# First graph layer: one product sum of 16 tiles a round, its turning and adding put into the next round

## The chip, the cores and the metric

One core of one Trainium2 chip runs the whole kernel. The metric is the device time of one execution in microseconds (us); lower is better. The engines are TensorE (PE, with its weight loads PEld), VectorE (DVE), ScalarE (ACT), GpSimd (POOL) and SyncE (SP), each with its own instruction stream; they meet at semaphores.

## The reference

Four graph layers run one after the other on 6250 nodes of 128 features and 206250 edges, sorted by destination node, and each ends in a residual add and a layer norm. Only the first layer (a graph attention layer with 4 heads of 32 channels) is touched:

```
h = (x @ W).reshape(n, 4, 32)
a_s = einsum('nhc,hc->nh', h, att_src);  a_d = einsum('nhc,hc->nh', h, att_dst)
e = leaky_relu(a_s[src] + a_d[dst], 0.2)
m = segment_max(e, dst);  p = exp(e - m[dst]);  z = segment_sum(p, dst)
out = segment_sum(h[src] * (p / z[dst])[:, :, None], dst)
```

## The kernel before

Edges are cut into tiles of 128 and rounds of 16 tiles; a round is 4 slots (b = 0 to 3) of 4 tiles. There are 101 rounds. All edges of a round fall on fewer than 128 neighbouring nodes, so the `narrow` branches run, and the rounds are written out one after another (`straight`). `par` is the round's number modulo 2.

- GpSimd (L621) fetches 16 tiles of source rows from the table in HBM by indirect DMA, into `g[par]`. The 16 DMAs of slot b = 0 to 3 wait for the product sum `agg` of the same slot of the round now finished: round i's sums free the buffer for the rows of round i + 2.
- ScalarE copies the 16 x 4 source scores of a round out of `g` into `alpha` (L727, after `g_ready`), and TensorE transposes them into `raw` (L671, semaphore `raw_t`).
- VectorE then makes the running maximum over each node's edges with scans, in steps that go back and forth between it and TensorE: scans L789 and L790, ends of tiles L792 and L793; TensorE L675; carries between tiles L799 to L804; TensorE L681; copy L809, scans L810 and L811, maximum L813; TensorE transposes it back (L689, L690); scores and weights L818 to L829. `seg` counts VectorE's steps, `carry_mm` counts TensorE's four answers of a round (L675, L681, L690, L697).
- In the gaps between these steps VectorE makes one-hot matrices (L749 for the next round's destination scores, L756 for the sums), and TensorE the next round's destination scores, `dst_scores(i + 1, b)`, L639: 4 matmuls a slot, one slot behind each of the four steps. A float32 matmul shows as two rows in the trace, so a slot is "x8".
- ScalarE exponentiates the weights (L729, L731, L732) and copies the destination scores (L720). VectorE multiplies the rows by the weights (L761, `messages`), and takes the rescale factors of the old sums from TensorE's L697 (L835).
- TensorE sums the round with one-hot matrices (L660, 4 matmuls a slot, `agg` after each). Slots 0 and 1 go into one half of a PSUM bank, 2 and 3 into the other. ScalarE copies each half to `by_node` (L738), TensorE turns it (`turn(i, h)`, L646 and L647), and VectorE adds it to the accumulator (`add_half`: L771 twice, with the rescaling, for h = 0; L768 for h = 1). All of this is done before the next round's L671 on TensorE and L789 on VectorE: turn(i, 0) stands between the sums of slots 2 and 3, turn(i, 1) behind them.
- SyncE loads the next rounds' destination rows (L572, 1 MB), windows (L538) and break marks (L578, L580).

Of the kernel before, what the change touches and what calls it, by code (L numbers as in the profile page):

```python
# [19 lines left out]
ALU = mybir.AluOpType  # L20
# [3 lines left out]
P = 128  # L24
N = 6250
E = 206250
KT = 4
SLOTS = 4
ROUND = KT * SLOTS
# [21 lines left out]
Z0 = 2 * H0 + 1  # L51
# [57 lines left out]
def build(nc, a, out):  # L109
    ctx = ExitStack()  # L110
    with ctx:
# [452 lines left out]
        def seg_base(i):  # L564
            return (i + 1) * STEPS

        with nc.Block() as block:
# [58 lines left out]
            def _(pe):  # L626
# [3 lines left out]
                def program(narrow):  # L630
# [12 lines left out]
                    def turn(i, h):  # L643
                        pe.wait_ge(node_copied, 2 * i + h + 1)
                        pe.wait_ge(acc_step, 3 * i + 7 + h)
                        nc.tensor.transpose(PS[0][:, h, 0:P], by_node[:, h, 0:P], ident[:, :])  # L646
                        nc.tensor.transpose(PS[0][0:Z0, h, P:2 * P], by_node[:, h, P:GW], ident[:, :]).then_inc(turned, 1)  # L647

                    def sums(i, b, par):
                        n = i * SLOTS + b  # L650
                        pe.wait_ge(oh_done, n + 1)
                        pe.wait_ge(msg_done, n + 1)
                        pe.wait_ge(weighed, 2 * i + 2)
                        if not narrow:
                            sum_bank_free(pe, acc_step, i, b, narrow)
                        for k in range(KT):
                            o, row_ = oh[:, b, k, :], g[:, par, b * KT + k, :]
                            bank, c, start, stop = sum_place(narrow, b, k)
                            if narrow:
                                m = nc.tensor.matmul(PS[1][:, bank, 0:GW], o, row_, start=start, stop=stop)  # L660
                            else:
                                nc.tensor.matmul(PS[bank][:, 0, c:c + P], row_[:, 0:P], o, start=start, stop=stop)
                                m = nc.tensor.matmul(PS[bank][0:Z0, 1, c:c + P], row_[:, P:GW], o, start=start, stop=stop)
                        m.then_inc(agg, 1)

                    def round_(j, i, par, last):
                        base = seg_base(i)
                        pe.wait_ge(alpha_kept, i + 1)
                        pe.wait_ge(seg, base)
                        met(pe, i)  # L670
                        nc.tensor.transpose(raw, alpha[:, :, :].rearrange(flat_q), ident[:, :]).then_inc(raw_t, 1)  # L671

# [3 lines left out]
                        if not last:  # L676
                            dst_scores(i + 1, 0)

# [22 lines left out]
                        for b in range(SLOTS):  # L701
                            sums(i, b, par)
                            if narrow and b == 2:
                                turn(i, 0)
                        if narrow:
                            turn(i, 1)

                    for b in range(SLOTS):
                        dst_scores(0, b)
                    rounds(pe, round_, narrow)  # L710
# [3 lines left out]
            def _(act):  # L714
# [7 lines left out]
                def program(narrow):  # L722
                    def round_(j, i, par, last):
                        for b in range(SLOTS):
                            act.wait_ge(g_ready[par][b], 16 * KT * (j + 1))
                        act.wait_ge(seg, seg_base(i))
                        nc.scalar.copy(alpha, g[:, par, :, P:P + H0]).then_inc(alpha_kept, 1)  # L727
                        act.wait_ge(seg, seg_base(i) + 20)
# [4 lines left out]
                        if not last:  # L733
                            keep_dst_scores(i + 1)
                        if narrow:
                            for h in range(2):
                                act.wait_ge(agg, i * SLOTS + 2 * h + 2 + AHEAD)
                                nc.scalar.copy(by_node[:, h, :], PS[1][:, h, 0:GW]).then_inc(node_copied, 1)  # L738

                    keep_dst_scores(0)  # L740
                    rounds(act, round_, narrow)
# [3 lines left out]
            def _(dve):  # L745
# [17 lines left out]
                def program(narrow):  # L763
                    def add_half(at, i, h):
                        dve.wait_ge(turned, 2 * i + h + 1)
                        dve.wait_ge(acc_step, 3 * i + 8 + 2 * h)
                        if h:
                            dve.tensor_tensor(at, at, PS[0][:, 1, 0:2 * P].rearrange("p (a n) -> p a n", a=2), ALU.add).then_inc(acc_step, 1)  # L768
                            return
                        for d in range(2):  # L770
                            dve.scalar_tensor_tensor(at[:, d, :], at[:, d, :], scale2[:, d:d + 1], PS[0][:, 0, d * P:(d + 1) * P], ALU.mult, ALU.add).then_inc(acc_step, 1)  # L771
# [8 lines left out]
                    def round_(j, i, par, last):  # L780
# [25 lines left out]
                        between(i, 1, last)  # L806

# [26 lines left out]
                        dve.wait_ge(carry_mm, 4 * i + 4)  # L834
                        s.link(dve.tensor_tensor(scale2, down_p, unit2[:, :], ALU.add))  # L835
# [3 lines left out]
                        if narrow:  # L839
                            at = acc2[:, :, bass.ds(first_node(dve, i * ROUND), P)]  # L840
                            for h in range(2):
                                add_half(at, i, h)
                            return
# [1468 lines left out]
```

## Time and profile before

| | |
|---|---|
| median of 3 runs | 11816.71 us (11815.05 to 11828.76) |
| profiled execution | 11788.6 us, span 11786.7 us |
| busy: PE, PEld, DVE, ACT, POOL | 55%, 47%, 41%, 15%, 52% |
| mean granted TensorE clock | 0.639 of full speed |

The profile is of one execution. Its page divides the span into 40 slices of about 295 us; the rounds of the first layer lie in the first eleven. PE records are starts of matmuls and modelled ends. "Idle" in a row is the time its engine did nothing before it, with what ended it; "remote" means a semaphore whose sender the profile doesn't name there, "issue" nothing that it shows.

### The profile page before, as it was taken

The page shows a single profiled execution, that of the slowest core. Times are in us where ns is not written, and L with a number is a line of the kernel's source. Part 1 is how long each engine was busy: PE and PEld are TensorE (multiplying, and loading weights), DVE is VectorE, ACT ScalarE, POOL GpSimd, SP SyncE. Part 2 cuts the span into 40 slices and gives each one's busy share as a digit, 9 for nine tenths or more (in the row PEclk, how much of TensorE's full clock was granted, in tenths as well). Part 3 has the DMA queues.
Part 4 walks back from the last instruction along what each step waited for, and adds up shares of the span by engine and source line. Part 5 has one row for each costly group of instructions (what it writes and reads, how often), then busy time and mean ns, then how long its engine had stood idle before and what let it go on. Part 6 is the DMA issues. An engine that isn't in the chain of part 4 may idle for free. (4 is left out here: it accounts for less than half of the span.)

```text
span 11786.7 us, 95611 instructions
## 1 busy us (share of the span) xinstructions
PE 6487.3 (55%) x31067; PEld 5541.6 (47%) x31067; DVE 4881.6 (41%) x10538; ACT 1784.6 (15%) x2785; POOL 6158.0 (52%) x6479
## 2 busy tenths in 40 slices
PE   4555555555435555555544445444443677777775
PEld 4444444444425555555434444444432455555553
DVE  4444444444552222222345555555555344444444
ACT  0000000000110000000110000000011444444443
POOL 4544544554216666666445555555530566666663
PEclk6666666666555555555566666666655677777776
DMA  4222222222111111111133433333320222222221
GB/s 132 72 75 74 73 75 75 72 75 75 42 26 55 54 55 55 54 55 54 44 123 121 124 121 119 121 120 122 120 69 1 65 62 61 61 60 61 62 61 38
DMA packets 388329, 878.63 MB, mean 75 GB/s; under 512 B 134341, under 2 KB 202872, under 8 KB 368224
## 3 DMA queue, kind: packets, MB, share of 16 engines
q0 software_dynamic: 232704, 536.56, 16.5%
q1 hardware_dynamic: 150242, 324.95, 8.3%
q10 hardware_dynamic: 4896, 11.01, 0.2%
q8 instruction: 258, 4.23, 0.1%
q14 instruction: 229, 1.88, 0.1%
HBM read 839.65 MB, written 32.40 MB: 74 GB/s over the span
## 5 line engine op out<-in xcount | busy, mean ns | idle before, releaser
L621 POOL DMA_INDIRECT PM<-gat_table,src_idx x1616 | 1529.1, 946 | 1579.9 <-PE ps L660 1070.4
L2081 POOL DMA_INDIRECT TMP<-schnet_table,src_idx x1616 | 1563.3, 967 | 1355.5 <-DVEq L2183 481.8
L1595 POOL DMA_INDIRECT PM<-hgt_kv_table,src_idx x1616 | 1531.4, 948 | 1371.3 <-PE ps L1627 752.0
L1153 POOL DMA_INDIRECT PM<-gcn_table,src_idx x1004 | 953.0, 949 | 463.8 <-issue 288.6
L1169 PE MATMUL ps<-rows,xT 16*128 16x8 f32 x3232 | 625.6, 301 | 716.3 <-issue 696.0
L1169 PEld LDWEIGHTS ps<-rows,xT 16*128 16x128 f32 x3232 | 646.2, 277 | 702.8 <-issue 671.7
L1153 POOL DMA_INDIRECT TMP<-gcn_table,src_idx x612 | 578.6, 945 | 702.4 <-POOLq L1016 373.9
L2108 PE MATMUL ps<-PM 128*128 128x128 f32 x3232 | 627.8, 357 | 539.6 <-issue 402.7
L2108 PEld LDWEIGHTS ps<-PM 128*128 128x128 f32 x3232 | 571.7, 266 | 582.3 <-issue 581.9
L1627 PE MATMUL ps<-PM 128*128 128x136 f32 x3232 | 608.8, 353 | 337.5 <-DVE PM L1716 322.1
L1228 DVE TENSOR_TENSOR AC<-AC,ps 128x128 f32 x101 | 29.2, 289 | 1829.8 <-remote 1437.0
L639 PE MATMUL ps<-PM 128*128 128x4 f32 x3232 | 697.6, 339 | 101.9 <-issue 71.9
L1627 PEld LDWEIGHTS ps<-PM 128*128 128x128 f32 x3232 | 557.8, 253 | 374.6 <-DVE PM L1702 345.1
L639 PEld LDWEIGHTS ps<-PM 128*128 128x128 f32 x3232 | 662.3, 304 | 134.1 <-issue 90.1
L1610 PE MATMUL ps<-TMP 128*128 128x128 f32 x3232 | 654.2, 367 | 59.0 <-issue 24.4
L660 PE MATMUL ps<-PM 128*128 128x137 f32 x3232 | 644.2, 377 | 0.3 <-issue 0.3
L1610 PEld LDWEIGHTS ps<-TMP 128*128 128x128 f32 x3232 | 585.5, 271 | 91.0 <-issue 37.8
L2153 DVE TENSOR_TENSOR PM<-ps,TMP 128x512 f32<-128x512 f32 x404 | 277.2, 686 | 830.9 <-remote 609.4
L660 PEld LDWEIGHTS ps<-PM 128*128 128x128 f32 x3232 | 618.7, 281 | 3.0 <-issue 0.3
L2091 PE MATMUL ps<-PM,WA 50*128 50x512 f32 x808 | 595.3, 825 | 11.1 <-DMA PM<-in_attrT 11.1
L689 PE MATMUL ps<-ident,TMP 64*128 64x64 f32 x101 | 36.8, 365 | 1011.3 <-DVE TMP L813 844.4
L2098 PEld LDWEIGHTS ps<-WA,PM 128*128 128x128 f32 x3232 | 566.2, 246 | 35.8 <-issue 14.8
(374 smaller groups left out, 10772.4 us busy)
## 6 DMA issues: line engine op xcount, KB each, us to landing
PM<-local_dst_row SPq DMA_DIRECT2D x101, 1024.0 KB
PM<-local_dst_row SPq DMA_DIRECT2D x202, 512.0 KB
PM<-in_attrT SPq DMA_DIRECT2D x101, 400.0 KB
PM<-gat_table,src_idx POOLq DMA_INDIRECT x1616
PM<-hgt_kv_table,src_idx POOLq DMA_INDIRECT x1616
TMP<-schnet_table,src_idx POOLq DMA_INDIRECT x1616
PM<-gcn_table,src_idx POOLq DMA_INDIRECT x1004
xT<-in_rel_row SPq DMA_DIRECT2D x101, 128.0 KB
```

The costliest lines, as they stand in the source:

```text
L621: pool.indirect_dma_start(out=g[:, par, t, 0:ROW0], out_offset=None, in_=tab0_d, in_offset=bass.IndirectOffsetOnAxis(ap=src_idx[:, i * ROU ...
L639: m = nc.tensor.matmul(adp[:, t * H0:(t + 1) * H0], ohT[:, b % 2, k * P:(k + 1) * P], window_of(narrow, adw, i, b, k), start=True, stop=True)
L660: m = nc.tensor.matmul(PS[1][:, bank, 0:GW], o, row_, start=start, stop=stop)
L1153: pool.indirect_dma_start(out=g[n % DEEP][:, k, :], out_offset=None, in_=tab1_d, in_offset=bass.IndirectOffsetOnAxis(ap=src_idx[:, n * KT ...
L1169: m = nc.tensor.matmul(rel_ps[par][:, t, :], oh16[kind_rows(par), t * P:(t + 1) * P], rel_rows[kind_rows(par), :], start=True, stop=True)
L1595: pool.indirect_dma_start(out=g[:, par, t, 0:2 * P], out_offset=None, in_=kv_d, in_offset=bass.IndirectOffsetOnAxis(ap=src_idx[:, i * ROUN ...
L1610: m = nc.tensor.matmul(q_ps[b % 2][:, k, :], ohT[:, b % 2, k * P:(k + 1) * P], window_of(narrow, qw, i, b, k), start=True, stop=True)
L1627: m = nc.tensor.matmul(sums_ps, o, row_, start=b % 2 == 0 and k == 0, stop=b % 2 == 1 and k == KT - 1)
L2081: pool.indirect_dma_start(out=g[:, b, k, :], out_offset=None, in_=tab3_d, in_offset=bass.IndirectOffsetOnAxis(ap=src_idx[:, (i * SLOTS + b ...
L2091: nc.tensor.matmul(zb[b], w1, attr[:, par, b * KT * P:(b + 1) * KT * P], start=True, stop=True).then_inc(z_mm, 1)
L2098: m = nc.tensor.matmul(wb[b % 2][:, k, :], soft[:, b % 2, k * P:(k + 1) * P], w2, start=False, stop=(k == KT - 1), skip_group_check=True)
L2108: m = nc.tensor.matmul(sb_[bank][:, c:c + P], msg[:, b % 2, k, :], oh[:, b % 2, k, :], start=start, stop=stop)
```

## The change

The four slots of a round are summed into one PSUM region (`PS[1][:, par]`) as one sum of 16 tiles; ScalarE copies it once, `turn` and the add are done once a round. They move into the next round: TensorE's `turn(i - 1)` stands behind L675 and `dst_scores(i + 1, 0)`, VectorE's `add_round(i - 1)` behind its second `between` and ahead of the wait of L809. The transposition of the next round's scores (`scores_t(i + 1)`, with its wait for `alpha`) stands between the sums of slots 1 and 2, and ScalarE copies the next round's `alpha` (`keep_alpha`) before it waits for the sums. VectorE waits for the previous round's add before it writes the new rescale factors (L835). The last round turns and adds at its own end.

```diff
-                    def turn(i, h):
-                        pe.wait_ge(node_copied, 2 * i + h + 1)
-                        pe.wait_ge(acc_step, 3 * i + 7 + h)
-                        nc.tensor.transpose(PS[0][:, h, 0:P], by_node[:, h, 0:P], ident[:, :])
-                        nc.tensor.transpose(PS[0][0:Z0, h, P:2 * P], by_node[:, h, P:GW], ident[:, :]).then_inc(turned, 1)
+                    def turn(i, par):
+                        pe.wait_ge(node_copied, i + 1)
+                        pe.wait_ge(acc_step, 2 * i + 6)
+                        nc.tensor.transpose(PS[0][:, par, 0:P], by_node[:, par, 0:P], ident[:, :])
+                        nc.tensor.transpose(PS[0][0:Z0, par, P:2 * P], by_node[:, par, P:GW], ident[:, :]).then_inc(turned, 1)
+
+                    def scores_t(i):
+                        pe.wait_ge(alpha_kept, i + 1)
+                        pe.wait_ge(seg, seg_base(i))
+                        met(pe, i)
+                        nc.tensor.transpose(raw, alpha[:, :, :].rearrange(flat_q), ident[:, :]).then_inc(raw_t, 1)
...
-                                m = nc.tensor.matmul(PS[1][:, bank, 0:GW], o, row_, start=start, stop=stop)
+                                m = nc.tensor.matmul(PS[1][:, par, 0:GW], o, row_, start=b + k == 0, stop=b + k == SLOTS + KT - 2)
...
-                        pe.wait_ge(alpha_kept, i + 1)
-                        pe.wait_ge(seg, base)
-                        met(pe, i)
-                        nc.tensor.transpose(raw, alpha[:, :, :].rearrange(flat_q), ident[:, :]).then_inc(raw_t, 1)
-
...
                         if not last:
                             dst_scores(i + 1, 0)
+                        if narrow and i > 0:
+                            turn(i - 1, 1 - par)
...
                             sums(i, b, par)
-                            if narrow and b == 2:
-                                turn(i, 0)
-                        if narrow:
-                            turn(i, 1)
+                            if b == 1 and not last:
+                                scores_t(i + 1)
+                        if narrow and last:
+                            turn(i, par)
...
-                    def round_(j, i, par, last):
+                    def keep_alpha(j, i, par):
                         for b in range(SLOTS):
                             act.wait_ge(g_ready[par][b], 16 * KT * (j + 1))
-                        act.wait_ge(seg, seg_base(i))
                         nc.scalar.copy(alpha, g[:, par, :, P:P + H0]).then_inc(alpha_kept, 1)
...
                             keep_dst_scores(i + 1)
+                            keep_alpha(j + par, i + 1, 1 - par)
                         if narrow:
-                            for h in range(2):
-                                act.wait_ge(agg, i * SLOTS + 2 * h + 2 + AHEAD)
-                                nc.scalar.copy(by_node[:, h, :], PS[1][:, h, 0:GW]).then_inc(node_copied, 1)
+                            if i >= 2:
+                                act.wait_ge(turned, i - 1)
+                            act.wait_ge(agg, i * SLOTS + SLOTS + AHEAD)
+                            nc.scalar.copy(by_node[:, par, :], PS[1][:, par, 0:GW]).then_inc(node_copied, 1)
...
-                    def add_half(at, i, h):
-                        dve.wait_ge(turned, 2 * i + h + 1)
-                        dve.wait_ge(acc_step, 3 * i + 8 + 2 * h)
-                        if h:
-                            dve.tensor_tensor(at, at, PS[0][:, 1, 0:2 * P].rearrange("p (a n) -> p a n", a=2), ALU.add).then_inc(acc_step, 1)
-                            return
+                    def add_round(i, par):
+                        at = acc2[:, :, bass.ds(first_node(dve, i * ROUND), P)]
+                        dve.wait_ge(turned, i + 1)
+                        dve.wait_ge(acc_step, 2 * i + 8)
                         for d in range(2):
-                            dve.scalar_tensor_tensor(at[:, d, :], at[:, d, :], scale2[:, d:d + 1], PS[0][:, 0, d * P:(d + 1) * P], ALU.mult, ALU.add).then_inc(acc_step, 1)
+                            dve.scalar_tensor_tensor(at[:, d, :], at[:, d, :], scale2[:, d:d + 1], PS[0][:, par, d * P:(d + 1) * P], ALU.mult, ALU.add).then_inc(acc_step, 1)
...
                         between(i, 1, last)
+                        if narrow and i > 0:
+                            add_round(i - 1, 1 - par)
...
                         dve.wait_ge(carry_mm, 4 * i + 4)
+                        if narrow:
+                            dve.wait_ge(acc_step, 2 * i + 8)
                         s.link(dve.tensor_tensor(scale2, down_p, unit2[:, :], ALU.add))
...
                         if narrow:
-                            at = acc2[:, :, bass.ds(first_node(dve, i * ROUND), P)]
-                            for h in range(2):
-                                add_half(at, i, h)
+                            if last:
+                                add_round(i, par)
                             return
```

## Rows read from the trace of the kernel before

**Rows 1.** The page, part 2: busy tenths in 40 slices of the span.
```profile
PE   4555555555435555555544445444443677777775
DVE  4444444444552222222345555555555344444444
POOL 4544544554216666666445555555530566666663
PEclk6666666666555555555566666666655677777776
```

**Rows 2.** Waits, 200 to 2900 us: waiting engine and line, releaser, total us, times, longest.
```profile
DVE TMP L809 <- remote: 862.8, 85, 12.4
POOL PM L621 <- PE ps L660: 954.8, 93, 12.3
DVE AC L771 <- PE ps L647: 212.6, 48, 4.9
DVE AC L771 <- issue: 183.2, 41, 5.2
DVE AC L768 <- PE ps L647: 108.3, 54, 3.6
DVE AC L768 <- issue: 62.2, 34, 3.5
```

**Rows 3.** Timeline, GpSimd's first fetch of the 5th and of the 99th round.
```profile
203.57 0.94 POOL L621 DMA_INDIRECT PM<-gat_table,src_idx  x1 [12.20 <-PE ps L660]
...
3061.33 0.95 POOL L621 DMA_INDIRECT PM<-gat_table,src_idx  x1 [9.81 <-PE ps L660]
```

**Rows 4.** Timeline of one round, 625 to 657 us: start, us, instruction, count, idle before.
```profile
626.29 0.95 POOL L621 DMA_INDIRECT PM<-gat_table,src_idx  x1 [9.59 <-PE ps L660]
...
629.16 1.10 PE L660 MATMUL ps<-PM 128*128 128x137 f32 x8
629.46 0.61 DVE L771 SCALAR_TENSOR_TENSOR AC<-AC,TMP,ps 128x128 f32 x2 [4.42 <-PE ps L647]
630.56 0.28 ACT L738 COPY TMP<-ps 128x137 f32<-128x137 f32 x1 [2.40 <-PE ps L660]
...
631.36 0.42 DVE L768 TENSOR_TENSOR AC<-AC,ps 128x256 f32 x1 [1.29 <-PE ps L647]
632.02 0.41 DVE L789 TENSOR_TENSOR_SCAN TMP<-PM,ps 64x128 f32<-64x128 f32 x1 [0.23 <-PE ps L671]
...
633.19 0.22 PE L675 MATMUL ps<-TMP,head_of 64*4 64x32 f32 x2 [1.76 <-DVE TMP L792]
...
633.78 1.05 PE L639 MATMUL ps<-PM 128*128 128x4 f32 x8 [0.37 <-issue]
...
634.26 0.13 DVE L799 COPY TMP<-TMP 4x1 f32<-4x1 f32 x1
...
634.78 0.28 DVE L804 TENSOR_TENSOR TMP<-TMP,ident 4x128 f32<-4x128 f32 x1
...
635.12 0.54 PE L681 MATMUL ps<-ones,TMP 4*64 4x1 f32 x4 [0.28 <-issue]
...
645.04 0.94 POOL L621 DMA_INDIRECT PM<-gat_table,src_idx  x1 [0.30 <-issue]
647.61 0.15 DVE L809 COPY TMP<-ps 64x2 f32<-64x2 f32 x1 [11.34 <-remote]
...
650.08 0.13 DVE L818 TENSOR_TENSOR TMP<-TMP,ps 4x1 f32<-4x1 f32 x1
...
653.17 0.14 DVE L835 TENSOR_TENSOR TMP<-ps,unit 128x2 f32<-128x2 f32 x1
...
656.58 0.95 POOL L621 DMA_INDIRECT PM<-gat_table,src_idx  x1 [10.60 <-PE ps L660]
```

**Rows 5.** Timeline of a round whose L675 came early, 2515 to 2546 us.
```profile
2515.55 0.95 POOL L621 DMA_INDIRECT PM<-gat_table,src_idx  x1 [12.10 <-PE ps L660]
...
2523.28 0.58 PE L681 MATMUL ps<-ones,TMP 4*64 4x1 f32 x4 [0.18 <-issue]
...
2529.82 0.15 DVE L809 COPY TMP<-ps 64x2 f32<-64x2 f32 x1 [5.40 <-remote]
...
2538.32 0.14 DVE L818 TENSOR_TENSOR TMP<-TMP,ps 4x1 f32<-4x1 f32 x1 [5.95 <-remote]
...
2544.83 0.95 POOL L621 DMA_INDIRECT PM<-gat_table,src_idx  x1 [9.53 <-PE ps L660]
```

**Rows 6.** Timeline of a round whose L681 came late, 2361 to 2396 us.
```profile
2361.05 0.95 POOL L621 DMA_INDIRECT PM<-gat_table,src_idx  x1 [9.64 <-PE ps L660]
...
2375.04 0.58 PE L681 MATMUL ps<-ones,TMP 4*64 4x1 f32 x4
...
2384.10 0.15 DVE L809 COPY TMP<-ps 64x2 f32<-64x2 f32 x1 [7.92 <-remote]
...
2393.08 0.94 POOL L621 DMA_INDIRECT PM<-gat_table,src_idx  x1 [12.27 <-PE ps L660]
```

More of the change, by code:

```diff
@@ L702, in round_ @@
                             sums(i, b, par)
-                            if narrow and b == 2:
-                                turn(i, 0)
-                        if narrow:
-                            turn(i, 1)
+                            if b == 1 and not last:
+                                scores_t(i + 1)
+                        if narrow and last:
+                            turn(i, par)
                     for b in range(SLOTS):
                         dst_scores(0, b)
+                    scores_t(0)
                     rounds(pe, round_, narrow)
@@ L722, in program, with round_ @@
                 def program(narrow):
-                    def round_(j, i, par, last):
+                    def keep_alpha(j, i, par):
                         for b in range(SLOTS):
                             act.wait_ge(g_ready[par][b], 16 * KT * (j + 1))
-                        act.wait_ge(seg, seg_base(i))
                         nc.scalar.copy(alpha, g[:, par, :, P:P + H0]).then_inc(alpha_kept, 1)
+                    def round_(j, i, par, last):
                         act.wait_ge(seg, seg_base(i) + 20)
@@ L734, in round_ @@
                             keep_dst_scores(i + 1)
+                            keep_alpha(j + par, i + 1, 1 - par)
                         if narrow:
-                            for h in range(2):
-                                act.wait_ge(agg, i * SLOTS + 2 * h + 2 + AHEAD)
-                                nc.scalar.copy(by_node[:, h, :], PS[1][:, h, 0:GW]).then_inc(node_copied, 1)
+                            if i >= 2:
+                                act.wait_ge(turned, i - 1)
+                            act.wait_ge(agg, i * SLOTS + SLOTS + AHEAD)
+                            nc.scalar.copy(by_node[:, par, :], PS[1][:, par, 0:GW]).then_inc(node_copied, 1)
                     keep_dst_scores(0)
+                    act.wait_ge(seg, seg_base(0))
+                    keep_alpha(0, 0, 0)
                     rounds(act, round_, narrow)
```

## Prediction, written before the changed kernel was built or run

> **What bounds the kernel now.** I read the page's slices first, then the waits of the first layer, then its timeline round by round. The chain that ended last is of no use here: it ends in the fourth layer. In the slices no engine of the first eleven is full: PE and GpSimd stand at 4 to 5 tenths and TensorE is granted 0.6 of its speed [rows 1]. So the layer is bound by a chain that goes from engine to engine, and its length per round is what counts. The first fetch of the 5th and of the 99th round are 3061.33 - 203.57 = 2857.76 us apart: 94 rounds of 30.40 us [rows 3].
>
> The waits say where those go. Per round VectorE waits some 10 us at the copy L809 (862.8 us, 85 times), and 6 us for the turned sums: 212.6 + 183.2 + 108.3 + 62.2 = 566 us at L771 and L768 over 89 rounds. GpSimd waits 10 us for the sums, 954.8 us in 93 waits [rows 2]. A reader who takes these at face value sees 6 us a round to win by moving the turn away. The timeline says that it is less simple.
>
> I count from the first fetch of a round (F). In the ordinary round [rows 4] F is 626.29. The turned sums hold VectorE until 631.78; the scans start at F + 5.7, L675 at F + 6.9, L681 at F + 8.8. L681's record ends at F + 9.4 and nothing else stands before the copy L809, yet this starts at F + 21.3. The fetches run from F to F + 19.7 (last at 645.04, 0.94 us). From L809 to the next F the chain takes 8.97 us, from L818 6.50 us, from L835 3.41 us.
>
> The wait at L809 is the strange part. Twelve PE rows (8 of L639's slot 0, 4 of L681) are recorded between F + 7.5 and F + 9.4, but their answer is there only at F + 21.3: from L681's start 12.5 us, or 1.04 us a row, while the fetches run. Earlier in the same fetches answers come at once: L675 at 633.19 lets L799 start at 634.26. The Trainium skill ("Perfetto Trace Analysis", Summary: the profiler window per engine type) says that a TensorE record's end is an estimate and that semaphore propagation is hidden from it; the trace agrees, since L809 comes 11.9 us after L681's recorded end.
>
> How does the wait depend on when L681 comes? In an early round [rows 5] L681 is at F + 7.7, L809 at F + 14.3: 1.1 us earlier in, 7.0 us earlier out. But then L818 waits 5.95 us, until F + 22.8, and the next F is at F + 29.3. In a late round [rows 6] L681 is at F + 14.0, L809 at F + 23.05, the next F at + 32.0. So there is a shadow over TensorE's answers from about F + 7.5 to about F + 22.8: what enters before it is prompt, what enters it crawls, and all is out soon after the fetches end. The period is the time at which the shadow lets go plus the chain that is still undone then: 21.3 + 9.0 = 30.3, 22.8 + 6.5 = 29.3, 23.05 + 9.0 = 32.0.
>
> **The change part by part.**
> Moved off the head of the round: both turns, their adds and the copies. VectorE is free for the scans as soon as the transposed scores are there. These come behind the sums of slot 1; the three slots behind the first end at 629.16 + 1.10 = F + 4.0, so slot 1 ends near F + 2 and the scans can start near F + 2.3 instead of F + 5.7. `alpha` doesn't hold it: its copy stands behind ScalarE's L720 and needs rows that were fetched a round earlier.
> But L675 stands in TensorE's queue behind the sums of slot 3, so it comes at F + 4.1, or some tenths later with the extra transposition in between, against F + 6.9. L804 comes 1.59 us behind L675 (633.19 to 634.78), lasts 0.28, and lets L681 start: F + 6.1 against F + 8.8. That is 2.7 us earlier, and out of the 6 us that the waits seemed to offer.
>
> Added before L681 on TensorE: `turn`, behind slot 0 of L639. It waits for the copy of `by_node`, which started 0.3 us behind the sums (630.56), so it is there at F + 4.6; L639's slot 0 takes 1.05 us from F + 4.5. The turn costs two transpositions, about 0.3 us by the nearest rows. If it falls in the shadow it costs its 2 to 4 rows at 1.04 us, so 2 to 4 us. I take 0.3, since it is issued near F + 5.6.
> Added before L809 on VectorE: two rows of 0.61 us together, as L771. VectorE is idle there now. If that cover goes they cost 0.61 us; queued behind are L809 to L813, and TensorE's L689 waits for those. One add of 0.42 us (L768), one copy of 0.28 us on ScalarE and two transpositions go away for good. All lie beside the wait: 0.
> The wait before L835 is for adds made some 15 us earlier: 0; were it real, the messages of slots 1 to 3 and the sums would queue behind it. DMAs: none is added or moved; SyncE's and GpSimd's lists are as before. The sums keep their 16 matmuls and an `agg` a slot, so the fetches start by the same rule.
>
> Where does the new round meet the shadow? By F + 7.5 slot 0 of L639, the turn and L681 (F + 6.1 to 6.7) are in. L809 then lies between 6.8 (prompt) and 14.3 (the early round); I take F + 8.5, nearer the prompt end since L681 is 1.6 us ahead of the early round's. What is next late is L818: it needs slot 1 of L639 (8 rows), L689 (1) and L690 (2). Eleven rows at 1.04 are 11.4 us: F + 20. The shadow's end, F + 22.8, is the upper bound. I take the middle, F + 21.4, and 6.5 us behind it: period 27.9 us.
> The sum: (27.9 - 30.4) x 100 rounds = -250 us. The bounds: L818 at F + 22.8 gives 29.3 (-110 us). If L690 too got out early, the shadow would hold slot 2 of L639 and L697, and let go at 22.8 with L835's 3.4 us to do: 26.2 (-420 us).
> The span 11786.7 becomes 11537; the profiled execution took 11788.6, 28 us less than the median of the runs, 11816.7, which becomes 11567.
>
> **The rivals.**
> *A, the full shadow (29.3 us a round, -110 us, 11707).* L818's answer is held to F + 22.8 as in the early round [rows 5]. For it: that round had L809 at 14.3 and still paid. Against: there L690 was entered about F + 16, in the new order near F + 10.
> *B, more gets through (26.2, -420 us, 11397).* Against: 11 rows would have to pass in far less than 1.04 us each.
> *C, the wait isn't tied to the fetches but to the products, and keeps its 12.5 us.* Then L809 moves with L681 by 2.7 us: 27.7, -270 us, 11547. The late round speaks against it, with 9.1 us. The Trainium skill ("SBUF — State Buffer", Who interferes with whom) says that only the port pair of VectorE and GpSimd contends and that DMA never contends with a compute engine; by that rule this rival would be the right one. No row names what holds TensorE's answers.
> *D, swallowed.* The shadow depends on how much TensorE has done since F, not on when. The new order has the same 24 rows of sums and 8 of slot 0 ahead of L681, so L809 stays at F + 21.3: 30.4, 0 us, 11817. The early round speaks against it: same work, 7 us sooner.
> *E, slower.* The turn waits in the shadow: if slot 0 of L639 is held, the turn behind it adds its 2 to 4 us ahead of L681, and VectorE's add stands ahead of L809. It decides if L681's answer comes later than F + 21.3; then L809 goes to the late round's 23.05 and the period to 32.0: +160 us, 11977. For it: the turn was prompt between the sums, and its new place is 3 us nearer to the shadow.
> The change does do what it says: the narrow branch runs, since `turn` has records.
>
> **How the numbers follow.** Forecast 0.40, A 0.15, B 0.12, C 0.11, D 0.10, E 0.12. 0.2% is 24 us, about what a measurement can tell from no change. Faster: 0.40 + 0.15 + 0.12 + 0.11 = 0.78; same 0.10; slower 0.12. The range leaves out E and a tail beyond B: 11380 to 11830; B and D lie inside. The forecast's own range is 11420 to 11680 (26.5 to 29.1 us).
>
> **What would show it.** The scans L789 should start near F + 2.3, L675 near F + 4.3, L681 near F + 6.3. The idle time before L809 should shrink from 10 us a round to 2 or 3, and that before L818 rise to 8 or more; L768 is gone; the first fetches should stand 27.9 us apart. GpSimd's wait for L660 should fall from 10 to 8 us. The other layers should be the same. I am wrong if L809 still comes at F + 21 (D, E), or if L818 does not wait and the wait has gone to L835 or the sums (B).

## The result and the profile after

The changed kernel takes 11733.34 us (median of 4, 11731.05 to 11745.68), the kernel before on the same chip 11820.16 us: ratio 0.9926, interval 0.9914 to 0.9938, 87 us less. Forecast were 250 us less (11567). The sign was right, the size was not; 87 us lies nearest to rival A (110).

The profiled execution took 11745.68 us, its span 11743.3. GpSimd's first fetches of two rounds, 92 rounds apart (for the kernel before: [rows 3]):

```profile
201.04 0.94 POOL L621 DMA_INDIRECT PM<-gat_table,src_idx  x1 [12.17 <-PE ps L666]
...
2941.93 0.94 POOL L621 DMA_INDIRECT PM<-gat_table,src_idx  x1 [12.20 <-PE ps L666]
```

2740.89 / 92 = 29.79 us a round against 30.40: 0.61 x 100 = 61 us of the 87. In these two profiled executions the second layer's first fetch comes at 3419.8 us instead of 3486.3, so 66 us earlier, but the spans differ by 43 us only: the third layer, which the change doesn't touch, took 17 us longer. About 20 us either way lies in the other layers from one execution to the next.

Lines have moved (before -> now): L671 -> L653, L789 -> L796, L675 -> L676, L799 -> L806, L681 -> L684, L809 -> L818 (the copy of the carries), L818 -> L827 (the scores), L835 -> L846. The sums are now L666, the add L778. Note that L818 names the scores in the old kernel and the copy of the carries in the new one. Below, "the carries" and "the scores" mean the moment at which VectorE goes on with TensorE's answer. One ordinary round of the changed kernel, timeline, against [rows 4]:

```profile
1512.61 0.94 POOL L621 DMA_INDIRECT PM<-gat_table,src_idx  x1 [12.18 <-PE ps L666]
...
1514.25 0.41 DVE L796 TENSOR_TENSOR_SCAN TMP<-PM,ps 64x128 f32<-64x128 f32 x1 [2.88 <-issue]
...
1516.03 0.22 PE L676 MATMUL ps<-TMP,head_of 64*4 64x32 f32 x2
1516.17 1.05 PE L639 MATMUL ps<-PM 128*128 128x4 f32 x8
...
1518.31 0.14 DVE L806 COPY TMP<-TMP 4x1 f32<-4x1 f32 x1 [1.75 <-remote]
...
1519.24 0.39 PE L684 MATMUL ps<-ones,TMP 4*64 4x1 f32 x4 [1.53 <-DVE TMP L811]
...
1524.86 0.61 DVE L778 SCALAR_TENSOR_TENSOR AC<-AC,TMP,ps 128x128 f32 x2 [4.48 <-remote]
...
1528.31 0.15 DVE L818 COPY TMP<-ps 64x2 f32<-64x2 f32 x1 [2.85 <-remote]
...
1535.38 0.14 DVE L827 TENSOR_TENSOR TMP<-TMP,ps 4x1 f32<-4x1 f32 x1 [4.52 <-remote]
...
1541.90 0.94 POOL L621 DMA_INDIRECT PM<-gat_table,src_idx  x1 [9.57 <-PE ps L666]
```

Read from the first fetch F = 1512.61: the scans start at F + 1.6, L676 at F + 3.4, L684 at F + 6.6, close to the forecast (2.3, 4.3, 6.3). But VectorE already waits 1.75 us for L676's answer, the turned sums come at F + 12.3, the carries (L818) at F + 15.7, and the scores (L827) at F + 22.8. The chain behind L827 is 6.5 us as before, and the next F is at 29.3. One long wait was cut into four. Over the 92 rounds the medians are F + 5.7 for L806, 17.2 for the carries and 22.9 for the scores; the carries range from 10.8 to 23.0, but the scores never come before F + 22.7.

The trace also keeps the time at which each semaphore was raised, which no view above prints. In this round TensorE's answers arrive in the order of its instructions: L676's at F + 5.7, the turn's at 12.1, L684's at 15.7, that of L639's slot 1 at 22.70, the scores' at 22.75 and that of slot 2 at 22.84. From L676 to L684 stand 14 matmul rows (8 of slot 0, 2 of the turn, 4 of L684): 10.0 us, so 0.7 us a row; the 8 rows of slot 1 take another 7.0 us, 0.9 us a row. Then the 8 rows of slot 2, of which each has its own record at F + 17.7 to 19.6, are answered 0.1 us behind slot 1's and the scores'. Eight such rows took 1.05 us at best here (L639 at 1516.17), so these had been computed before and only their answer was held, behind the answers ahead of it.

Some rounds take 31 to 32 us. This is the round just before the one above:

```profile
1480.73 0.95 POOL L621 DMA_INDIRECT PM<-gat_table,src_idx  x1 [9.56 <-PE ps L666]
...
1488.94 0.39 PE L684 MATMUL ps<-ones,TMP 4*64 4x1 f32 x4 [1.47 <-DVE TMP L811]
...
1503.63 0.15 DVE L818 COPY TMP<-ps 64x2 f32<-64x2 f32 x1 [2.81 <-remote]
...
1506.11 0.13 DVE L827 TENSOR_TENSOR TMP<-TMP,ps 4x1 f32<-4x1 f32 x1
```

L684 comes at F + 8.2 and the carries at F + 22.9, so the scores at 25.4: 31.9 us. Of 92 rounds 72 took 29.3 to 29.6 us, and 15 took 31.1 to 31.9. All 15 are among the 23 rounds, every fourth, at whose start SyncE also loads L578. The waits from 200 to 2900 us, against [rows 2]:

```profile
POOL PM L621 <- PE ps L666: 918.9, 93, 12.2
DVE AC L778 <- remote: 486.7, 84, 11.6
...
DVE TMP L818 <- remote: 334.9, 84, 5.7
DVE TMP L827 <- remote: 215.5, 60, 9.4
```

### The profile page after: what moved, and what is told of

It reads as the page before. It is cut to its first block and busy times, and to the rows that moved or that the text cites. A ratio compares the mean times of both kernels' runs of the same rounds, so it can differ in the third digit from the quotient of the medians.

```text
span 11743.3 us, 95003 instructions
## 1 busy us (share of the span) xinstructions
PE 6312.4 (54%) x30865; PEld 5385.9 (46%) x30865; DVE 4855.6 (41%) x10437; ACT 1759.6 (15%) x2684; POOL 6154.7 (52%) x6479
## 3 DMA queue, kind: packets, MB, share of 16 engines
q0 software_dynamic: 232704, 536.56, 17.7%
## 5 line engine op out<-in xcount | busy, mean ns | idle before, releaser
L2118 PEld LDWEIGHTS ps<-PM 128*128 128x128 f32 x3232 | 567.1, 264 | 586.1 <-issue 585.8
L1637 PEld LDWEIGHTS ps<-PM 128*128 128x128 f32 x3232 | 560.6, 254 | 342.0 <-DVE PM L1712 317.6
L639 PE MATMUL ps<-PM 128*128 128x4 f32 x3232 | 614.7, 313 | 81.4 <-DVE PM L758 59.7
L666 PE MATMUL ps<-PM 128*128 128x137 f32 x3232 | 633.8, 372 | 0.3 <-issue 0.3
L639 PEld LDWEIGHTS ps<-PM 128*128 128x128 f32 x3232 | 579.5, 269 | 107.8 <-DVE PM L758 72.4
L666 PEld LDWEIGHTS ps<-PM 128*128 128x128 f32 x3232 | 610.5, 277 | 4.1 <-issue 0.3
L2101 PE MATMUL ps<-PM,WA 50*128 50x512 f32 x808 | 587.3, 815 | 12.3 <-DMA PM<-in_attrT 12.3
```

Source lines behind the costliest of these rows:

```text
L639: m = nc.tensor.matmul(adp[:, t * H0:(t + 1) * H0], ohT[:, b % 2, k * P:(k + 1) * P], window_of(narrow, adw, i, b, k), start=True, stop=True)
L666: m = nc.tensor.matmul(PS[1][:, par, 0:GW], o, row_, start=b + k == 0, stop=b + k == SLOTS + KT - 2)
L1637: m = nc.tensor.matmul(sums_ps, o, row_, start=b % 2 == 0 and k == 0, stop=b % 2 == 1 and k == KT - 1)
L2101: nc.tensor.matmul(zb[b], w1, attr[:, par, b * KT * P:(b + 1) * KT * P], start=True, stop=True).then_inc(z_mm, 1)
L2118: m = nc.tensor.matmul(sb_[bank][:, c:c + P], msg[:, b % 2, k, :], oh[:, b % 2, k, :], start=start, stop=stop)
```

## The experiments

The runs stand in six groups, each beside runs of the kernel before. This took 11674 us in the first group (e1 to e4), 9295, 9304 and 9286 us in the next three (e5 to e8, e9 to e12, e13 and e14), 11823 and 11848 us in the last two (e15 and e16, e17 and e18). Each run is compared with the kernel before of its own group. In what follows the hold is the lateness of TensorE's answers under fetches; the groups of 11674 us and more have it, those of about 9300 us don't. The expectations speak of chips with and without the hold. But the record numbers the chip 0 both in the group of e1 to e4, with the hold, and in that of e9 to e12, without it, so whether it belongs to a chip, to its machine or to a state of either isn't shown.

**Without fetches, new and old order.** Rounds 2 to 100 fetch nothing and work on stale rows.

```diff
+                        if i >= 2:
+                            continue
                         for k in range(KT):
...
-                            act.wait_ge(g_ready[par][b], 16 * KT * (j + 1))
+                            act.wait_ge(g_ready[par][b], 16 * KT)
```

> The changed kernel without the indirect fetches of rounds 2 to 100 of the first layer (those rounds work on the rows of the first two; nothing else is left out). Theory 'the fetches hold TensorE's answers': the waits before the copy of the carries (L818 in the changed kernel) and before the next scores go away; the carries are copied about 7 us after the round's first sum and the chain of 9.0 us follows, so 16.2 us a round instead of 29.8, total near 10370 us. Rival 'the wait belongs to TensorE's products themselves': 29 to 30 us a round, total within 1% of 11733 us.

> The kernel before without the indirect fetches of rounds 2 to 100 of the first layer. Theory 'the fetches hold TensorE's answers': carries copied at about 9.9 us, then 9.0 us: 18.9 us a round instead of 30.4, total near 10670 us; against the changed kernel without fetches that gives what the new order is worth where nothing holds the answers, 2.7 us a round or 270 us, three times the 87 us measured with fetches. Rival 'the products': 30.4 us a round. If the two kernels without fetches lie within 90 us of each other, the gain was lost to something else than the fetches.

Measured: 10246 us (new order) and 10529 us (old), against 11674 us for the kernel before. Timelines, new and old (the lines are shifted by 2):

```profile
1007.02 0.39 PE L686 MATMUL ps<-ones,TMP 4*64 4x1 f32 x4
1008.33 0.14 DVE L820 COPY TMP<-ps 64x2 f32<-64x2 f32 x1
1010.78 0.13 DVE L829 TENSOR_TENSOR TMP<-TMP,ps 4x1 f32<-4x1 f32 x1
```

```profile
1008.82 0.58 PE L683 MATMUL ps<-ones,TMP 4*64 4x1 f32 x4 [0.28 <-DVE TMP L806]
1009.89 0.14 DVE L811 COPY TMP<-ps 64x2 f32<-64x2 f32 x1
1012.35 0.13 DVE L820 TENSOR_TENSOR TMP<-TMP,ps 4x1 f32<-4x1 f32 x1
```

The carries come 1.1 to 1.3 us after the start of their product, without a wait (medians of all rounds: 1.5 and 1.1), where they took 9 to 12.5 us under fetches. So the answers are late only when GpSimd fetches; rival C is out. And the new order is worth 283 us where nothing holds them (2.7 us a round were expected; the first layer ends 281 us sooner). The change does what its order says; the hold takes most of it.

**Half of the fetches**, and **as many fetches of an eighth of the bytes**.

```diff
+                            if i >= 2 and k >= 2:
+                                continue
```

> The changed kernel with 2 of 4 indirect fetches in each slot from round 2 on (half of the rows are stale). The fetches then end near 10 us after the round's first sum instead of 19.8. Theory 'held until the fetches end': the wait before the scores ends near 13 us instead of 22.8, and with 6.5 us behind it the round takes about 19.5 us, total near 10700 us. Rival 'a hold of fixed length once fetches begin': 29.3 us. Rival 'each fetch adds its own delay to the answers': the waits shrink by half, about 22 us a round.

```diff
+                            w = 17 if i >= 2 else ROW0
-                            pool.indirect_dma_start(out=g[:, par, t, 0:ROW0], out_offset=None, in_=tab0_d,
+                            pool.indirect_dma_start(out=g[:, par, t, 0:w], out_offset=None, in_=tab0_d if w == ROW0 else tab0_d.rearrange("n (a f) -> (n a) f", f=w),
```

> The changed kernel with the same number of indirect fetches but 68 bytes of each row instead of 544 (the rest is stale). If the moving of bytes holds TensorE's answers: waits gone or small, near 17 us a round until GpSimd's 16 issues of 1.25 us bound it at 20 to 21 us, total near 10850 us. If GpSimd's making of the fetches holds them: no change, 29.8 us a round, total near 11733 us.

Half of the fetches: 10752.82 us, a single run. One of its rounds:

```profile
1011.50 0.94 POOL L623 DMA_INDIRECT PM<-gat_table,src_idx  x1 [10.64 <-PE ps L668]
...
1016.61 0.39 PE L686 MATMUL ps<-ones,TMP 4*64 4x1 f32 x4 [0.21 <-issue]
1020.24 0.94 POOL L623 DMA_INDIRECT PM<-gat_table,src_idx  x1 [0.30 <-issue]
1022.86 0.15 DVE L820 COPY TMP<-ps 64x2 f32<-64x2 f32 x1 [1.43 <-remote]
1025.33 0.13 DVE L829 TENSOR_TENSOR TMP<-TMP,ps 4x1 f32<-4x1 f32 x1
...
1031.83 0.94 POOL L623 DMA_INDIRECT PM<-gat_table,src_idx  x1 [10.65 <-PE ps L668]
```

The last fetch is issued at F + 8.7 and ends at 9.7; the carries come at F + 11.4; 20.3 us a round (mean of 91 rounds: 20.5). The hold ends with the fetches, not after a fixed time. The rival by which each fetch adds its own delay asked for 22 us, the hold to the end of the fetches for 19.5; the measured 20.5 lies between them, nearer the second. With short rows the hold stays: 11631.86 us (also a single run), against 11733 x 11674 / 11820 = 11589 us, which the changed kernel would take in this group by its ratio. Its rounds take 29.4 us and its scores come at F + 22.7, as in the changed kernel (29.8 and 22.9). So the bytes of the rows have no visible part in it. What is left is what goes with the number of fetches and rows: GpSimd's issue of them, their descriptors, or their own signals of completion. No run tells these apart.

**Plain loads by SyncE** of as many bytes into the same buffers, in place of the indirect fetches (other rows, so other data).

```diff
+                            for b in range(SLOTS):
+                                sp.wait_ge(agg, i * SLOTS + b + 1 + 2 * SLOTS)
+                                for k in range(KT):
+                                    t = b * KT + k
+                                    r = (i * ROUND + t) % 48 * P
+                                    sp.dma_start(g[:, par, t, 0:ROW0], tab0_d[r:r + P, :]).then_inc(p_ready[par][b], 16)
```

> The changed kernel with the 16 indirect fetches of rounds 2 to 100 replaced by 16 plain loads of 128 rows of 544 bytes each, issued by SyncE behind the same sums (same bytes, fixed rows, so other data). If GpSimd's making of the fetches holds TensorE's answers: the waits go away as without fetches, 15.4 us a round or what SyncE's issues and the loads need, total below 10500 us. If writes into these buffers or the traffic hold them: 25 us a round or more, total above 11200 us.

> Plain loads by SyncE once more. On a chip with the hold: if GpSimd's making of the fetches holds TensorE's answers, there is no hold and the time is that of the other chip, 9834 us in the first layer's terms (the other three layers still fetch and are held: total 10000 to 10600 us). If writes into the buffers hold them: above 11200 us.

Measured 9833.59 and 9821.81 us, where the kernel before took 9295 and 9304 us. They cost 539 and 518 us more there; the cause wasn't looked for. Both groups are without the hold, so this doesn't tell whether plain loads would cause it. Inconclusive.

**A quarter of the destination scores** (one of four matmuls in each slot of L639).

```diff
-                        for k in range(KT):
+                        for k in range(1 if narrow and i > 0 else KT):
```

> The changed kernel with 1 instead of 4 matmuls in each slot of the next round's destination scores (L639; three of four scores are left out from round 1 on). My prediction priced a matmul row in the shadow at 1.04 us. By that, 6 fewer rows ahead of L818 and 6 more ahead of L827 let the scores' wait end well before 22.8 us, the round then takes 26 us or less, total near 11350 us. Theory 'answers are held until the fetches end, whatever the rows': L818 comes sooner, L827 still at 22.8 us; the round is shorter only by the three matmuls saved in each of slots 2 and 3 behind it (2 x 1.4 us at most), 27 to 28.5 us, total 11450 to 11600 us.

> One of four matmuls in each slot of the destination scores once more. On a chip with the hold: by my 1.04 us a row, 26 us a round or less, total 380 us or more under the changed kernel. By 'held until the fetches end, whatever the rows': L827 still at 22.8 us and a round of 27 to 28.5 us, 130 to 280 us under it.

> One of four matmuls in each slot of the destination scores, for a chip with the hold. By my 1.04 us a row: 26 us a round or less. By 'held until the fetches end, whatever the rows': L827 still at 22.8 us, a round of 27 to 28.5 us. On a chip without the hold: 9300 us, no difference.

9318.72, 9305.11 and 9286.33 us, single runs against 9295, 9304 and 9286: within 0.3%, and again no hold in any of these groups. So this didn't test my price of 1.04 us a row.

**The changed kernel without the hold.**

> The changed kernel itself, for the chip that this call gets. Where the kernel before takes 11600 us or more (TensorE's answers are held while GpSimd fetches): ratio 0.9926 again. Where it takes 9300 us (no hold, the fetches bind the round at 20 us): ratio 1.000 within 0.1%, since what the new order saves is covered by the fetches.

9291.91 us against 9286.2: ratio 1.0007 (0.9997 to 1.0016). Its timeline:

```profile
1003.25 0.39 PE L684 MATMUL ps<-ones,TMP 4*64 4x1 f32 x4
1003.89 0.94 POOL L621 DMA_INDIRECT PM<-gat_table,src_idx  x1 [0.30 <-issue]
1004.40 0.14 DVE L818 COPY TMP<-ps 64x2 f32<-64x2 f32 x1
...
1018.57 0.41 DVE L796 TENSOR_TENSOR_SCAN TMP<-PM,ps 64x128 f32<-64x128 f32 x1 [6.45 <-PE ps L653]
```

Here the carries' answer takes 1.15 us in the midst of fetches (at most 1.53 us in 90 rounds). GpSimd issues one every 1.25 us without a pause, 16 x 1.25 = 20 us a round, and VectorE waits for the next scores, which wait for fetched rows. Here the first layer is bound by the fetches, and the new order has nothing to win.

**No turn and no add** (the sums are not accumulated).

```diff
-                        if narrow and i > 0:
-                            turn(i - 1, 1 - par)
...
-                        if narrow and i > 0:
-                            add_round(i - 1, 1 - par)
```

> The changed kernel without the turn (L646, L647) and the add (L778) in every round (the sums are not accumulated). If the turn in its new place delays the carries' answer and this sets the round (my rival E in small): 1 to 3 us a round less, total 11450 to 11650 us. If the hold's end sets the round: L818 comes 2 to 4 us sooner, but L827 stays at 22.8 us and the total stays within 0.4% of 11733 us, but for the rounds that took 31.9 us.

> No turn and no add once more. On a chip with the hold: if the turn sets the round, 100 to 300 us under the changed kernel. If the hold's end sets it: L818 2 to 4 us sooner, L827 still at 22.8 us, within 0.4% of the changed kernel but for the rounds of 31.9 us.

> No turn and no add, for a chip with the hold: if the turn in its new place sets the round, 100 to 300 us under the changed kernel's ratio of 0.9926, so 0.967 to 0.984; if the hold's end sets it, 0.989 to 0.993. Without the hold: 1.000.

Without the hold 9293.49 us (ratio 0.9998, 0.9988 to 1.0008) and 9301.02 us. With it 11679.42 us against 11822.74: 0.988 (0.986 to 0.990). One round of it, and a rare one, timeline:

```profile
1010.56 0.94 POOL L621 DMA_INDIRECT PM<-gat_table,src_idx  x1 [9.76 <-PE ps L666]
...
1024.14 0.15 DVE L810 COPY TMP<-ps 64x2 f32<-64x2 f32 x1 [5.81 <-remote]
1033.34 0.14 DVE L819 TENSOR_TENSOR TMP<-TMP,ps 4x1 f32<-4x1 f32 x1 [6.65 <-remote]
```

```profile
577.57 0.94 POOL L621 DMA_INDIRECT PM<-gat_table,src_idx  x1 [9.57 <-PE ps L666]
...
586.13 0.15 DVE L810 COPY TMP<-ps 64x2 f32<-64x2 f32 x1 [2.43 <-remote]
...
594.67 0.14 DVE L819 TENSOR_TENSOR TMP<-TMP,ps 4x1 f32<-4x1 f32 x1 [6.00 <-remote]
...
601.18 0.94 POOL L621 DMA_INDIRECT PM<-gat_table,src_idx  x1 [3.90 <-PE ps L666]
```

In the first, ordinary one the carries come at F + 13.6, 2.1 us sooner than in the round shown of the changed kernel (median of 93 rounds: 12.8 against 17.2), and the scores still at F + 22.8. Most of what is saved comes from the slow rounds: none takes over 30.5 us. So in an ordinary round the turn delays the carries and costs nothing; it helps to push some of every fourth over the edge.

But F + 22.8 is not a fixed time. In nine of the 93 rounds the scores come clearly before it: seven times at F + 21.3 or 21.4 (27.8 to 28.0 us a round) and twice at F + 17.1 and 17.8, as in the second one (23.6 and 24.4 us), while GpSimd's last fetch ends at F + 19.7. All nine had their carries by F + 10.8, and in the seven the 11 rows ahead of the scores then took 10.6 to 12.0 us, so 1.0 to 1.1 us a row, which is my price (0.8 in the two). The nine together are worth about 21 us. So answers do pass under the fetches, at a price for each row, and the end of the fetches is the latest time, which lets go whatever is still held.

**A shorter tail.** TensorE's slot 3 of L639 behind the sums of slot 0, VectorE's multiplication of slot 0 ahead of the last one-hots.

```diff
-                        if not last:
+                        if not last and not narrow:
                             dst_scores(i + 1, 3)
...
                             sums(i, b, par)
+                            if b == 0 and narrow and not last:
+                                dst_scores(i + 1, 3)
...
-                        between(i, 3, last)
                         s.settle()
                         dve.wait_ge(weighed, 2 * i + 2)
                         messages(i, 0, par)
+                        between(i, 3, last)
```

> The changed kernel with the chain behind the hold shortened: TensorE's slot 3 of L639 stands behind the sums of slot 0 instead of ahead of them, and VectorE multiplies the rows of slot 0 before it makes the one-hot matrices of slot 3 (nothing left out). Theory 'a round is 22.8 us of hold and the chain behind it': the sums of slot 0 start 1.4 to 1.6 us sooner, each round takes 27.8 to 28.0 us instead of 29.4, total 0.9873 of before less 1.2%: 140 to 160 us under the changed kernel, ratio to before 0.979 to 0.982. Rival 'the round is held to 29.3 us by something periodic (the fetches' 20 us and the loads behind them)': no change, ratio 0.9926.

> The short tail once more. The chip of the first try ran the kernel before in 9295 us: there nothing holds TensorE's answers, the fetches bound the round at 20 us and the tail is covered. On a chip where the kernel before takes 11600 us or more: theory 'hold to 22.8 us plus the chain behind it' gives 27.8 to 28.0 us a round, ratio to before 0.979 to 0.982; rival 'held to 29.3 us by something periodic' gives 0.9926. On a chip like the first: ratio 1.000.

> The short tail, for a chip with the hold (kernel before above 11600 us): 'hold to 22.8 us plus the chain behind it' gives 27.8 to 28.0 us a round and a ratio to before of 0.979 to 0.982; 'held to 29.3 us by something periodic' gives 0.9926. On a chip without the hold: 1.000.

Without the hold the ratios are 1.0006 and 1.0005. With it 11793.44 us against 11822.74: 0.9977 (0.9967 to 0.9986). That is slower than the changed kernel's 0.9926, and both theories missed. One round:

```profile
1201.22 0.94 POOL L621 DMA_INDIRECT PM<-gat_table,src_idx  x1 [10.62 <-PE ps L666]
...
1210.73 0.39 PE L684 MATMUL ps<-ones,TMP 4*64 4x1 f32 x4
1223.96 0.15 DVE L820 COPY TMP<-ps 64x2 f32<-64x2 f32 x1
...
1226.44 0.13 DVE L829 TENSOR_TENSOR TMP<-TMP,ps 4x1 f32<-4x1 f32 x1
...
1231.45 0.94 POOL L621 DMA_INDIRECT PM<-gat_table,src_idx  x1 [10.57 <-PE ps L666]
```

The chain behind the scores fell as meant, from 6.5 to 1231.45 - 1226.44 = 5.0 us. But the 8 rows of slot 3 now stand at the head of the fetches. L684 comes at F + 9.5, and it is the carries' answer that is held to F + 22.7. The scores come 2.5 us behind it: 30.2 us (mean of 90 rounds: 30.4). The round has the shape of the kernel before again.

**The break marks first**, and **slot 3 last**. SyncE loads the marks right behind L572; in the second also slot 3 of L639 behind all sums, with the short tail's VectorE order.

```diff
+                            sp.wait_ge(seg, i * STEPS + 12)
+                            load_breaks(i + 1, 1 - par)
                             sp.wait_ge(ad_mm, i * SLOTS + SLOTS + 2)
                             load_round_window(sp, i + 2, adw, tab0_d[:, P + H0:ROW0], ad_ready)
```

> The changed kernel with SyncE's list in another order: the break marks (L578, L580) are loaded right behind the destination rows, 3 us ahead of the fetches instead of up to 0.5 us into them (nothing left out). In the changed kernel every fourth round, the one with L578, takes 31.2 to 31.9 us and the others 29.3 to 29.5. If the loads in the fetches' first microsecond delay the first answers, and so push the carries' answer to 22.9 us and the scores' to 25.4 us: these rounds fall to 29.4 us, 40 to 55 us less, ratio to before 0.988 to 0.989 on a chip with the hold. If they are slow for another reason: 0.9926. On a chip without the hold: 1.000.

```diff
+                        if narrow and not last:
+                            dst_scores(i + 1, 3)
                         if narrow and last:
                             turn(i, par)
...
+                            if not narrow:
+                                keep_dst_scores(i + 1)
                             keep_alpha(j + par, i + 1, 1 - par)
+                            if narrow:
+                                keep_dst_scores(i + 1)
```

> The same, and TensorE's slot 3 of L639 behind all sums of the round (the short tail had it between the sums of slots 0 and 1, where it pushed L676 from 3.8 to 6.4 us and so the carries' answer back to 22.8 us); ScalarE copies alpha ahead of the destination scores, VectorE multiplies slot 0 ahead of the last one-hots. Theory 'a round is the hold's end plus the chain behind the last answer held': L676 stays under 5 us, the scores' answer stays at 22.8 us, the chain behind it takes 5.0 us as in the short tail instead of 6.5: 27.8 to 28.0 us a round, ratio to before 0.974 to 0.980 on a chip with the hold. If the mended tail isn't kept: 0.988 or more. On a chip without the hold: 1.000.

Break marks first: 11699.9 us against 11848.42, ratio 0.9871 (0.9854 to 0.9887), the fastest version that computes everything. Two of its first fetches, 65 rounds apart, so 29.32 us a round:

```profile
1019.02 0.95 POOL L625 DMA_INDIRECT PM<-gat_table,src_idx  x1 [9.66 <-PE ps L670]
...
2925.13 0.94 POOL L625 DMA_INDIRECT PM<-gat_table,src_idx  x1 [9.66 <-PE ps L670]
```

No round of 93 takes over 29.5 us. The marks' loads are now issued from F - 4.1 to F - 2.3, in the changed kernel from F - 1.2 to F + 0.2, and SyncE's other loads stay where they were. So loads of the marks this close to the first fetches were needed for the slow rounds; e16 shows that without the turn they aren't enough. They delay the ordinary round too: the median of L676's answer goes from F + 5.7 to 4.3, that of the carries from 17.2 to 15.7. How a load does that, and whether L578 alone would do it, isn't shown. Slot 3 last: 11824.44 us, ratio 0.998 (0.9971 to 0.999). One round:

```profile
1026.43 0.94 POOL L625 DMA_INDIRECT PM<-gat_table,src_idx  x1 [11.28 <-PE ps L670]
1031.59 0.22 PE L680 MATMUL ps<-TMP,head_of 64*4 64x32 f32 x2
1037.27 0.58 PE L688 MATMUL ps<-ones,TMP 4*64 4x1 f32 x4 [2.02 <-DVE TMP L820]
1049.75 0.14 DVE L827 COPY TMP<-ps 64x2 f32<-64x2 f32 x1
```

L680 came at F + 5.2 where I expected under 5, the product of the carries (L688) only at F + 10.8, and the carries at F + 23.3: 30.6 us a round in the mean, where 27.8 to 28.0 were expected. The expectation for the tail fell a second time, and in the same way: with slot 3 at the head of the fetches the carries themselves are held to the end.

## Why the prediction was right or wrong

- **The shadow over TensorE's answers while GpSimd fetches: right**, and now shown: it is gone without the fetches (e1, e2), and ends sooner with half of them (e3). **Its end at F + 22.8, with 6.5 us behind L827: right** in the changed kernel (22.8 and 29.3), though as the latest time and not a fixed one (e16).
- **The new times of the scans, L675 and L681: right** within 0.9 us (1.6, 3.4, 6.6 against 2.3, 4.3, 6.3). The 2.7 us a round that this should be worth is what e1 and e2 show, 283 us.
- **The step that failed is where the new round meets the shadow.** I took it that all is prompt up to F + 7.5, so the carries at F + 8.5, and from there 11 rows at 1.04 us to F + 20, averaged with the upper bound to 21.4. Measured were F + 15.7 for the carries in the round shown (median 17.2) and 22.8 for the scores. The price of a row was about right (0.7 to 0.9 us in the round shown, 1.0 to 1.1 in seven rounds of e16), but it also holds for the rows that I had let through free: slot 0 of L639, the turn and L684, 14 rows from F + 5.7 on. With the carries at 17.2 and 11 rows behind them the scores run into the end of the fetches, so the upper bound was the forecast to make. That is 1.4 us of the 2.5 us a round that I forecast. Answers are late already at F + 5.7, where in the old order they were prompt at F + 8.0 [rows 4]. The early round [rows 5] gave the hint: L809 earlier by 7 us and the period at the same 29.3 us.
- So **rival A** happened in the ordinary round: 29.3 us would be 110 us less. It lacks the rounds of 31 to 32 us, which the old order had too [rows 6] and for which my sum has no term. They are worth 29.79 - 29.32 = 0.47 us a round, which e17 gave back. With them 61 us come from the rounds, and the rest of the 87 us lies within what the other layers vary.
- **Rival C: out** (e1, e2). **Rival D**, that the carries stay at F + 21.3: out, they came at 15.7.
- **Rival E**, the turn in the shadow: the turn does wait there (its answer comes at F + 12.1) and the carries behind it come later for it (median 17.2 against 12.8 without turn and add), but the end of the fetches swallows that in most rounds. What is left is small (e16: 0.988 against 0.9926), most of it in the slow rounds.
- **The turn and add at 0, VectorE's wait before L835 at 0: right** for the ordinary round; VectorE waits 2.8 us for the carries behind its add.
- That the hold can be absent was in no case of mine. Without it all versions that compute everything lie within 0.1% of the kernel before.

## What to carry to other kernels

When one event ends all waits (here the end of the fetches), making one answer earlier moves the wait to the next answer. Unless so little is left in the stretch that all of it passes before that event, as in nine rounds of e16, count a gain only up to the event plus the chain behind it, and look for a round in the old profile that already shows that case. If a price holds for some rows of a stretch, charge it to all of them before you let any through free. What stands at the head of such a stretch matters: 8 matmul rows moved into it cost more than they saved outside (e15, 0.9977 against 0.9926), and a few loads moved out of it gained 0.5% (e17, 0.9871). An order tuned in one place should be timed in others: here it was worth 0.7% in one and nothing in another.

## What the runs showed of the hardware that was not expected

- Three groups ran the same kernel before in 9286 to 9304 us, four measurements elsewhere gave 11674 to 11848 us. In the changed kernel L684 to L818 takes 1.15 us amid fetches in the one kind and 9.1 us (1519.24 to 1528.31; median 11.2) in the other. Of the 2455 us between its two traces (e13 and the result) 970 lie in the first layer's stretch of fetches and 1460 in those of the other three layers, almost nothing outside them. That the late answers cause it is shown for the first layer; in the others it fits, but their waits weren't read. The fetches themselves are no slower: a packet of 4352 bytes takes 289 ns with the hold and 287 ns without.
- The hold doesn't depend on the bytes of a fetch (68 or 544 a row), and ends 1.7 to 3.1 us after GpSimd's last fetch (e3, and the changed kernel). It delays the answers of TensorE, in their order, and, for the rows of slot 2 at least, not the computing of them. What holds the answers, and why in some groups only, stays open: that GpSimd's descriptor work does it was argued from e4 and not shown, since plain loads were only tried where there is no hold.
